# Spline and causal phases: TensorE multiplies the identity with the tokens into an unread bank at seven places

## The chip, the cores and the metric

The kernel runs on one core of a Trainium2 chip. The metric is the device time in microseconds of one execution, a median over runs. All data are float32.

## What is computed

A two-layer network over 4 x 512 tokens of 128 values. Layer 0 is half a mixture-of-experts step, a relative-position attention with 16 heads, and the mixture step again. Layer 1, on which the change bears, is cut here to its spline step and its causal step:

```python
# spline step, twice, around the causal step: x = x + 0.5 * spline(layernorm(x))
cluster_idx = argmax(calibrate(xf @ cluster_sigs.T))        # 8 clusters
sel_gates   = calibrate(xf @ sigs.T)[cluster_idx]           # 8 tiles of the chosen cluster
tile_idx    = cluster_idx * 8 + argmax(sel_gates)
comp = tanh(gelu(xf @ compress_w1 + b1) @ compress_w2 + b2)
hh   = relu(comp @ spline_w1[tile_idx] + spline_b1[tile_idx])
mag  = hh @ spline_w2[tile_idx] + spline_b2[tile_idx]
y    = layernorm(xf + mag * directions[tile_idx] * output_scale)
# causal step: x = x + causal(layernorm(x))
k, q = rotate(x @ Wk + bk), rotate(x @ Wq + bq)
wei  = softplus(causal_mask(k @ q.T / sqrt(128)))
out  = (wei @ (x @ Wv + bv)) @ Wp + bp
```

## The kernel before, in words

All tokens lie in SBUF as `x`, 16 tiles of 128 tokens by 128 values. `network` runs the phases one after the other: the layer-0 phases up to about 622 us of the profile, then `spline_phase` ("l1f0"), `causal_phase` ("l1a"), and `spline_phase` again ("l1f1"; the profile shows both spline phases under the name l1f). Each phase is a block with its own program for each engine; the engines meet at a barrier between phases. Within a phase the order on each engine is the order in which the code is written, and engines wait for one another at counted semaphores (`wait_ge`).

**A spline phase** on TensorE: `turn_tiles` transposes four normalised tiles (L2145), `score` multiplies each with 72 columns of cluster and tile signatures (L2151), `squeeze` makes the 32 hidden values of a group of four tiles (L2155). This is done for groups 0 and 1 and then for groups 2 and 3. Then `compress` (L2161) makes the two compressed values, after ScalarE's Gelu (`h_ready`). `turn_hots` (L2169) transposes the one-hot choice of tile, and `pick_parameters` (L2176) multiplies it with the table of parameters, 193 columns for each token tile.

VectorE carries the long chain: statistics, `calibrate`, `choose` and `pick_cluster` on clusters for tiles 0 to 7 (half 0) and for tiles 8 to 15 (half 1); each `pick_cluster` raises `picks_ready`. Then `calibrate`, `choose` and `mark_tiles` on the picked gates of half 0 (which raises `hot_ready`), the addition of a bias to compress's result (it waits for `comp_psum`), the same for half 1, and `magnitude` and `move_along` for each half. `calibrate` begins at L2021 and waits for ScalarE's exponential of the scores; `magnitude` begins at L2065 and waits for `par_psum`, that is for `pick_parameters`. `turn_hots(0)` waits for `hot_ready`, and `turn_hots(2)` for its second count.

ScalarE copies the transposes out of PSUM, takes the exponentials, normalises tiles 8 to 15, and computes Gelu, which is queued behind the exponential of the first picked gates.

**The causal phase** handles four batches of four tiles: `turn` (L2413) transposes, `keys_and_queries` (L2421) makes keys (n = 0) and queries (n = 1) with two 128x512 matmuls each, `values` (L2428), `score` (L2436), `gather` (L2447). VectorE's `rotate` (L2346 to L2351) waits for `kq_psum` and makes `kT` and `qT`, for which TensorE's first `score` waits.

In the profile each float32 matmul is two instructions of TensorE, a transpose is one.

Of the kernel before, what the change touches and what calls it, by code (L numbers as in the profile page):

```python
# [192 lines left out]
def attention_dram(nc):  # L193

    def dram(n, shape, dt=F32):
        return nc.dram_tensor(n, shape, dt).ap()

    return {

        "stack": [dram(f"stacked_{n}", (MARGIN + B * HEADS * 32 * FAR_PITCH,)) for n in "qk"],  # L200

        "tab": [dram(f"position_{n}", (B, TAB_SPAN)) for n in "qk"],

        "near": dram("near_terms", (B, P, 64, WIN)),
    }


def clear_semaphores(nc, sems):
# [1640 lines left out]
def spline_phase(nc, name, x, consts, lw, out=None):  # L1849


    c = consts
    HALF = TILES // 2
    N = HALF * 8
    with ExitStack() as ctx:
# [5 lines left out]
        def sem(n):  # L1861
            own_sems.append(ctx.enter_context(nc.semaphore(f"{name}_{n}")))
            return own_sems[-1]
# [22 lines left out]
        banks = ctx.enter_context(nc.psum_tensor(f"{name}_banks", [P, 8, 512], F32))  # L1886
# [11 lines left out]
        clusters_ready, picks_ready, sigs_ready = sem("clusters_ready"), sem("picks_ready"), sem("tile_sigs_ready")  # L1898
# [11 lines left out]
        with nc.Block() as block:  # L1910
# [227 lines left out]
            def _(pe):  # L2138
                def turn_tiles(g):
                    if g >= 2:  # L2140
                        pe.wait_ge(xnT_ready, g - 1)
                    for k in range(4):
                        t = 4 * g + k
                        pe.wait_ge(*((xn_by_dve, t + 1) if t < HALF else (xn_by_act, t + 1 - HALF)))
                        last = pe.transpose(psT[:, g % 2, k, :], xn[:, t, :], c["ident"][:, :])  # L2145
                    last.then_inc(xnT_psum, 1)
# [11 lines left out]
                def compress():  # L2158
                    pe.wait_ge(h_ready, 1)
                    for k in range(4):  # L2160
                        last = pe.matmul(ps_comp[:, k, :, :].rearrange("p g o -> p (g o)"), hT[:, k, :],  # L2161
                                         lw.cw2[:, :, :].rearrange("p g o -> p (g o)"), start=True, stop=True)
                    last.then_inc(comp_psum, 1)

                def turn_hots(g):
                    pe.wait_ge(*((h_ready, 1) if g < 2 else (hotT_ready, g - 1)))
                    pe.wait_ge(hot_ready, g // 2 + 1)
                    for k in range(4):
                        last = pe.transpose(ps_hot[:, g % 2, k * P:(k + 1) * P], tile_hot[:, 4 * g + k, :], c["ident"][:, :])  # L2169
                    last.then_inc(hotT_psum, 1)  # L2170

                def pick_parameters(g):

                    pe.wait_ge(hotT_ready, g + 1)
                    for t in range(4 * g, 4 * g + 4):
                        last = pe.matmul(ps_par[:, t, :], tile_hotT[:, t, :], lw.table[:, :], start=True, stop=True)  # L2176
                        if t % 2:
                            last.then_inc(par_psum, 1)

                for g in range(2):  # L2180
                    turn_tiles(g)
                score(0)
# [7 lines left out]
                squeeze(2)  # L2190
                squeeze(3)
                pe.wait_ge(xnT_ready, 4)
                compress()
                turn_hots(0)
                turn_hots(1)
                pe.wait_ge(comp_in_ready, 1)
# [13 lines left out]
def causal_phase(nc, name, x, consts, lw):  # L2210

    c = consts
    T = S // P
    with ExitStack() as ctx:
# [24 lines left out]
        ps_out = ps("ps_out", [P, S])  # L2239
# [13 lines left out]
        with nc.Block() as block:  # L2253
# [153 lines left out]
            def _(pe):  # L2407
                def turn(b):
                    if b:
                        pe.wait_ge(v_ready, b)  # L2410
                    for t in range(T * b, T * b + T):
                        pe.wait_ge(*((xn_by_dve, t + 1) if b == 0 else (xn_by_act, t + 1 - T)))
                        last = pe.transpose(ps_turn[:, (t % T) * P:(t % T + 1) * P], xn[:, t, :], c["ident"][:, :])  # L2413
                    last.then_inc(xT_psum, 1)
# [24 lines left out]
                def gather(b):  # L2439
# [8 lines left out]
                                             start=(j == 0), stop=(j == i))  # L2448
                    last.then_inc(y_psum, 1)

                turn(0)
                keys_and_queries(0, 0)
                keys_and_queries(0, 1)
# [67 lines left out]
```

## Time and profile before

| | us |
|---|---|
| median of 3 runs | 779.23 (777.95 to 779.53) |
| span of the profiled execution | 801.8 |
| TensorE busy in it | 578.0 (72%) |
| VectorE busy | 532.2 (66%) |
| ScalarE busy | 436.6 (54%) |
| mean granted TensorE clock | 0.838 |

The span runs from the first to the last instruction of one execution that was profiled; no other time is given for that execution. It is longer than the median of the timed runs, so its durations serve for differences, not for the total. The granted clock is 1.00 at 2.4 GHz and 0.50 at 1.2 GHz. The profile is read here by stretches: 622.3 to 682.4 us is the first spline phase, 682.4 to 739.6 the causal phase, 739.6 to the end the second spline phase.

### The profile page before, as it was taken

To read this page: it belongs to the slowest core of one execution; us is meant where nothing else is said; L and a number is where in the kernel's file an instruction comes from. 1 tells how busy PE (TensorE), PEld (TensorE's weight loads), DVE (VectorE), ACT (ScalarE), POOL (GpSimd) and SP (SyncE) were. 2 spreads that over 40 slices of the span, in tenths; PEclk is the share of its full clock that TensorE was granted. 3 is DMA by queue.
4 is the path that set the end of the run, shared out by engine and by line. 5 is a ranking of instruction groups with operands and counts; after the bars stand their busy time and mean duration, and the time that the engine had idled before them with its cause. 6 is when DMAs were issued, how large, how long until landed. Compare 5 with 4: busy or idle time off the path is not lost. (4 is left out here: it accounts for less than half of the span.)

```text
span 801.8 us, 16622 instructions
## 1 busy us (share of the span) xinstructions
PE 578.0 (72%) x5220; PEld 415.4 (52%) x5220; DVE 532.2 (66%) x1878; ACT 436.6 (54%) x944; POOL 225.0 (28%) x280
## 2 busy tenths in 40 slices
PE   4238964666999999999999996431994752577660
PEld 3227961233656666676667665221993542255450
DVE  7511217645778877999999985750225789666887
ACT  2004533335788888888888883610651433465522
POOL 1742443300850680094310000063342200212100
PEclk9998996976999999999999997555997555799655
DMA  8627943999999999999954406413553000000001
GB/s 249 207 92 230 277 131 101 288 317 307 265 340 360 264 303 348 255 228 309 311 125 124 126 22 191 108 48 112 172 166 89 0 1 0 1 1 1 0 1 52
DMA packets 128945, 130.79 MB, mean 163 GB/s; under 512 B 27436, under 2 KB 105116, under 8 KB 127964
## 3 DMA queue, kind: packets, MB, share of 16 engines
q1 hardware_dynamic: 122204, 101.89, 46.2%
q0 software_dynamic: 4544, 26.79, 9.0%
q10 hardware_dynamic: 2112, 1.05, 0.5%
q8 instruction: 44, 0.72, 0.4%
q14 instruction: 41, 0.34, 0.1%
HBM read 73.43 MB, written 52.92 MB: 158 GB/s over the span
## 5 line engine op out<-in xcount | busy, mean ns | idle before, releaser
L1479 DVE CUSTOM_DVE_ANT_0 l0am_prob<-l0am_ps_s,l0am_bias 128x512 f32<-128x512 f32 x256 | 161.6, 687 | 46.9 <-PE l0am_ps_s L1556 36.0
L1399 ACT ACTIVATE l0am_prob<-l0am_prob,l0am_neg_top 128x512 f32<-128x512 f32 x256 | 172.2, 730 | 11.7 <-DVE l0am_neg_top L1479 11.7
L1568 PE MATMUL l0am_ps_t<-c_ident,l0am_prob 128*128 128x128 f32 x1024 | 138.2, 279 | 0.0
L1568 PEld LDWEIGHTS l0am_ps_t<-c_ident,l0am_prob 128*128 128x128 f32 x1024 | 113.9, 142 | 16.8 <-issue 15.9
L1393 ACT COPY l0am_probT<-l0am_ps_t 128x512 f32<-128x512 f32 x128 | 69.0, 590 | 44.0 <-PE l0am_ps_t L1568 44.0
L1466 DVE COPY l0am_probT<-l0am_ps_t 128x512 f32<-128x512 f32 x128 | 82.1, 682 | 2.5 <-PE l0am_ps_t L1568 2.4
L1556 PE MATMUL l0am_ps_s<-l0am_ks,l0am_qs 32*128 32x512 f32 x512 | 73.9, 647 | 13.3 <-DVE l0am_neg_top L1479 12.1
L767 DVE COPY l0f_xsT<-l0f_psT 128x128 f32<-128x128 f32 x46 | 13.4, 292 | 104.7 <-PE l0f_psT L875 76.9
L596 ACT ACTIVATE l0f_h<-l0f_psU,l0f_experts 128x128 f32<-128x128 f32 x184 | 52.5, 368 | 40.6 <-PE l0f_psU L885 24.3
L1581 PE MATMUL l0am_ps_c<-l0am_probT,l0am_v 128*9 128x128 f32 x2048 | 67.9, 273 | 0.9 <-issue 0.9
L512 POOL DMA_INDIRECT token_results<-l0f_ys,l0f_token_i x46 | 44.3, 964 | 82.6 <-DVE l0f_ys L777 80.2
L1172 POOL TENSOR_TENSOR l0am_near<-l0am_rows_q,l0am_rows_k 128x352 f32<-128x352 f32 (+7 forms) x24 | 31.3, 1334 | 98.7 <-DMA l0am_rows_k<-position_k 98.7
L885 PE MATMUL l0f_psU<-l0f_xsT,l0f_mine 128*128 128x128 f32 x368 | 54.4, 294 | 2.8 <-DVE l0f_xsT L767 1.5
L1581 PEld LDWEIGHTS l0am_ps_c<-l0am_probT,l0am_v 128*9 128x9 f32 x2048 | 49.5, 90 | 11.7 <-issue 11.6
L1181 POOL TENSOR_TENSOR l0am_near<-l0am_rows_q,l0am_rows_k 128x192 f32<-128x192 f32 (+6 forms) x96 | 54.0, 608 | 0.2
L885 PEld LDWEIGHTS l0f_psU<-l0f_xsT,l0f_mine 128*128 128x128 f32 x368 | 47.6, 202 | 6.4 <-DVE l0f_xsT L767 2.9
L502 POOL DMA_INDIRECT sorted_tokens<-l0f_xn,l0f_pos_i x32 | 31.4, 980 | 59.1 <-DVE l0f_pos_i L668 50.2
L1556 PEld LDWEIGHTS l0am_ps_s<-l0am_ks,l0am_qs 32*128 32x128 f32 x512 | 20.2, 184 | 39.2 <-issue 24.2
L875 PE MATMUL l0f_psT<-c_ident,l0f_xs 128*128 128x128 f32 x46 | 13.4, 292 | 28.5 <-DMA l0f_xs<-sorted_tokens 27.6
L1589 PEld LDWEIGHTS l0am_ps_g<-c_ident,l0am_headT 128*128 128x128 f32 x64 | 9.0, 140 | 48.1 <-issue 28.8
L1518 PE MATMUL l0am_ps_s<-l0am_xnT,l0w_wext 128*112 128x512 f32 (+1 forms) x48 | 26.2, 709 | 5.8 <-ACT l0am_rows L1375 5.1
L1375 ACT ACTIVATE l0am_rows<-l0am_ps_s,l0w_row_bias 112x512 f32<-112x512 f32 (+1 forms) x24 | 16.1, 687 | 21.9 <-DMA stacked_q<-l0am_rows 6.8
(314 smaller groups left out, 995.6 us busy)
## 6 DMA issues: line engine op xcount, KB each, us to landing
l0am_bias<-near_terms SPq DMA_DIRECT2D x128, 192.0 KB, 5.5
near_terms<-l0am_near POOLq DMA_DIRECT2D x6, 3072.0 KB, 13.1
l0f_mine<-l0f_experts SPq DMA_DIRECT2D x46, 256.0 KB
near_terms<-l0am_near SPq DMA_DIRECT2D x2, 3072.0 KB, 10.9
l0am_rows_k<-position_k SPq DMA_DIRECT2D x12, 448.0 KB, 8.1
position_q<-l0am_rows SPq DMA_DIRECT2D x20, 224.0 KB, 5.2
position_k<-l0am_rows SPq DMA_DIRECT2D x20, 224.0 KB, 5.3
l0f_experts<-in_L_ffn_w SPq DMA_DIRECT2D x2, 2048.0 KB, 9.2
```

Source lines behind the costliest of these rows:

```text
L502: pool.indirect_dma_start(xs_dram[:, :], bass.IndirectOffsetOnAxis(ap=pos_i[:, t:t + 1], axis=0), xn[:, t, 0:XS_COLS], None).then_inc(scat ...
L512: pool.indirect_dma_start(ys_dram[:, :], bass.IndirectOffsetOnAxis(ap=token_i[:, s:s + 1], axis=0), ys[:, s % UNROLL, :], None).then_inc(y ...
L596: last = nc.scalar.activation(h[:, j, k, :], psU[:, s % 2, k, :], ACT.Gelu_apprx_tanh, bias=part_of(row, SLAB_B1 + k, 1))
L885: last = pe.matmul(psU[:, s % 2, k, :], mine[:, j, k * P:(k + 1) * P], xsT[:, j, :], start=True, stop=True)
L1181: last = engine.tensor_tensor(view(near, at, (WIN + 1, 64), (1, width)), view(rows_q, ROW_OF[pq] * 64, (1, 64), (0, width)), view(rows_k, ...
L1393: nc.scalar.copy(probT[:, u // GROUP % 2, u % GROUP, :, :], ps_t[:, u % 2, :, :]).then_inc(copied_act, 1)
L1399: nc.scalar.activation(prob[:, k, :], prob[:, k, :], ACT.Exp, bias=neg_top[:, k:k + 1], scale=-1.0)\
L1466: dve.tensor_copy(probT[:, u // GROUP % 2, u % GROUP, :, :], ps_t[:, u % 2, :, :]).then_inc(copied_dve, 1)
L1479: dve.tensor_tensor_reduce(out=prob[:, k, :], in0=ps_s[:, j, :], in1=bias[:, j, at:at + S], scale=-1.0, scalar=HUGE, op0=ALU.add, op1=ALU.min,
L1556: pe.matmul(ps_s[:, j, :], qs[r, n % 2, t * P:t * P + P], ks[r, n % 2, :], start=True, stop=True, tile_position=(32 * j, 0)).then_inc(scor ...
L1568: last = pe.transpose(ps_t[:, u % 2, i, :], prob[:, u % SLOTS_, i * P:(i + 1) * P], ident[:, :])
L1581: last = pe.matmul(ps_c[32 * j:32 * j + DH + 1, 0:P], v[:, T4 * b + i, GROUP * g + j, :], probT[:, q % 2, j, i, :], start=(i == 0), stop=( ...
```

## The change

A helper `keep_busy` issues `count` float32 matmuls of the identity (stationary) with four tiles of the tokens `x` (512 moving columns). The result goes to a PSUM bank that nothing reads before it is overwritten: bank 6 in a spline phase, `ps_out` in the causal phase. They are issued where a phase opens (3 in a spline phase, 2 in the causal one), before `compress` (4) and before the first `turn_hots` (4). The last two places also get a wait for `picks_ready`, counts 1 and 2. Nothing else is changed; no other engine's program differs.

```diff
+def keep_busy(pe, bank, ident, x, count):
+    for _ in range(count):
+        pe.matmul(bank, ident[:, :], x[:, 0:4, :].rearrange("p t d -> p (t d)"), start=True, stop=True)
...
 (spline_phase, TensorE)
+                keep_busy(pe, banks[:, 6, :], c["ident"], x, 3)
                 for g in range(2):
                     turn_tiles(g)
                 score(0)
...
                 squeeze(3)
                 pe.wait_ge(xnT_ready, 4)
+                pe.wait_ge(picks_ready, 1)
+                keep_busy(pe, banks[:, 6, :], c["ident"], x, 4)
                 compress()
+                pe.wait_ge(picks_ready, 2)
+                keep_busy(pe, banks[:, 6, :], c["ident"], x, 4)
                 turn_hots(0)
                 turn_hots(1)
...
 (causal_phase, TensorE)
+                keep_busy(pe, ps_out[:, :], c["ident"], x, 2)
                 turn(0)
                 keys_and_queries(0, 0)
```

TensorE's program of the first spline phase before, in the order in which it is issued:

```order
1037 L2145 MATMUL l1f_banks<-c_ident,l1f_xn 128x128 x8
1038 L2151 MATMUL l1f_banks<-l1w_score_w,l1f_xnT 128x72 x8
1039 L2155 MATMUL l1f_banks<-l1f_xnT,l1w_cw 32x512 x2
1040 L2145 MATMUL l1f_banks<-c_ident,l1f_xn 128x128 x8
1041 L2151 MATMUL l1f_banks<-l1w_score_w,l1f_xnT 128x72 x8
1042 L2155 MATMUL l1f_banks<-l1f_xnT,l1w_cw 32x512 x2
1043 L2161 MATMUL l1f_banks<-l1w_cw,l1f_hT 128x8 x4
1044 L2169 MATMUL l1f_banks<-c_ident,l1f_tile_hot 64x128 x8
1045 L2176 MATMUL l1f_banks<-l1w_table,l1f_tile_hotT 128x193 x8
```

And now, with the line numbers of the changed kernel:

```order
1037 L212 MATMUL l1f_banks<-x_tokens,c_ident 128x512 x3
1038 L2152 MATMUL l1f_banks<-c_ident,l1f_xn 128x128 x8
1039 L2158 MATMUL l1f_banks<-l1w_score_w,l1f_xnT 128x72 x8
1040 L2162 MATMUL l1f_banks<-l1f_xnT,l1w_cw 32x512 x2
1041 L2152 MATMUL l1f_banks<-c_ident,l1f_xn 128x128 x8
1042 L2158 MATMUL l1f_banks<-l1w_score_w,l1f_xnT 128x72 x8
1043 L2162 MATMUL l1f_banks<-l1f_xnT,l1w_cw 32x512 x2
1044 L212 MATMUL l1f_banks<-x_tokens,c_ident 128x512 x4
1045 L2168 MATMUL l1f_banks<-l1w_cw,l1f_hT 128x8 x4
1046 L212 MATMUL l1f_banks<-x_tokens,c_ident 128x512 x4
1047 L2176 MATMUL l1f_banks<-c_ident,l1f_tile_hot 64x128 x8
1048 L2183 MATMUL l1f_banks<-l1w_table,l1f_tile_hotT 128x193 x8
```

The added matmuls are the three L212 rows; all others keep their order.

## Rows read from the trace of the kernel before

**Rows 1.** Busy time by stretch; PEclk (granted clock) stands after POOL.
```profile
627.30:642.40 15.10, 15.06 (x56) 10.26 (x56) 11.13 (x38) 8.48 (x20) 1.26 (x1) 0.50 0.00 0
...
652.40:667.20 14.80, 14.62 (x48) 12.49 (x48) 11.07 (x45) 5.62 (x9) 0.00 (x0) 0.50 0.00 1
...
692.40:738.20 45.80, 36.28 (x184) 24.58 (x182) 30.58 (x66) 26.40 (x61) 6.31 (x18) 1.00 0.00 1
```

**Rows 2.** Waits in the first spline phase: us in total, times, longest.
```profile
DVE l1f_terms L2065 <- PE l1f_banks L2176: 3.1, 2, 2.4
...
DVE l1f_plus L2021 <- ACT l1f_e L1945: 2.7, 2, 1.4
```

**Rows 3.** TensorE's timeline, first spline phase: start, us, line, shapes, instructions [idle before].
```profile
627.32 2.27 PE L2145 MATMUL l1f_banks<-c_ident,l1f_xn 128*128 128x128 f32 x8 [11.65 <-DVE l1f_xn L2091]
629.37 3.55 PE L2151 MATMUL l1f_banks<-l1w_score_w,l1f_xnT 128*128 128x72 f32 x16
...
643.28 1.85 PE L2161 MATMUL l1f_banks<-l1w_cw,l1f_hT 128*128 128x8 f32 x8 [0.90 <-ACT l1f_hT L1979]
652.49 1.89 PE L2169 MATMUL l1f_banks<-c_ident,l1f_tile_hot 128*64 128x128 f32 x8 [7.36 <-DVE l1f_tile_hot L2054]
654.31 5.51 PE L2176 MATMUL l1f_banks<-l1w_table,l1f_tile_hotT 64*128 64x193 f32 x16
```

**Rows 4.** VectorE's timeline, first spline phase, same columns.
```profile
622.35 0.87 DVE L2003 BATCH_NORM_STATS2 l1f_stats<-x_tokens 128x6 f32<-128x128 f32 x4 [1.04 <-PEq L214]
...
633.28 0.20 DVE L2021 TENSOR_SCALAR l1f_plus<-l1f_e 128x64 f32<-128x64 f32 x1 [1.44 <-ACT l1f_e L1945]
...
640.88 0.20 DVE L2021 TENSOR_SCALAR l1f_plus<-l1f_e 128x64 f32<-128x64 f32 x1 [1.23 <-ACT l1f_e L1945]
...
646.18 1.07 DVE L2049 TENSOR_REDUCE l1f_picks<-l1f_masked 128x64 f32<-128x512 f32 x1
...
651.65 0.69 DVE L2054 TENSOR_TENSOR l1f_tile_hot<-l1f_chosen 128x512 f32<-128x512 f32 x1
...
656.85 0.69 DVE L2054 TENSOR_TENSOR l1f_tile_hot<-l1f_chosen 128x512 f32<-128x512 f32 x1
```

**Rows 5.** TensorE's timeline, causal phase.
```profile
686.18 1.24 PE L2413 MATMUL l1a_ps_turn<-c_ident,l1a_xn 128*128 128x128 f32 x4 [19.07 <-DVE l1a_xn L2379]
688.10 5.83 PE L2421 MATMUL l1a_ps_kq<-l1a_xnT,l1w_w_kq 128*128 128x512 f32 x8 [0.68 <-ACT l1a_xnT L2271]
...
697.25 0.66 PE L2413 MATMUL l1a_ps_turn<-c_ident,l1a_xn 128*128 128x128 f32 x4 [2.44 <-DVE l1a_v L2357]
...
703.41 1.88 PE L2421 MATMUL l1a_ps_kq<-l1a_xnT,l1w_w_kq 128*128 128x512 f32 x4
```

**Rows 6.** VectorE's timeline: starts of the causal and second spline phase; wait for the first keys.
```profile
682.45 0.87 DVE L2328 BATCH_NORM_STATS2 l1a_stats<-x_tokens 128x6 f32<-128x128 f32 x4 [0.71 <-PEq L214]
...
691.91 0.75 DVE L2346 SCALAR_TENSOR_TENSOR l1a_straight<-l1a_ps_kq,l1w_b_kq,l1w_rope 128x512 f32<-128x512 f32 x1 [2.96 <-PE l1a_ps_kq L2421]
...
739.67 0.87 DVE L2003 BATCH_NORM_STATS2 l1f_stats<-x_tokens 128x6 f32<-128x128 f32 x4 [0.81 <-PEq L214]
```

**Rows 7.** TensorE's timeline, second spline phase.
```profile
744.63 2.27 PE L2145 MATMUL l1f_banks<-c_ident,l1f_xn 128*128 128x128 f32 x8 [6.50 <-DVE l1f_xn L2091]
...
754.17 2.00 PE L2151 MATMUL l1f_banks<-l1w_score_w,l1f_xnT 128*128 128x72 f32 x16
```

**Rows 8.** Single microseconds in which the granted clock moved.
```profile
692.00:693.00 1.00, 1.00 (x3) 0.29 (x3) 1.00 (x2) 0.00 (x0) 1.00 (x2) 0.80 0.00 0
740.00:741.00 1.00, 0.00 (x0) 0.00 (x0) 0.96 (x8) 0.92 (x1) 1.00 (x2) 0.60 0.07 16
760.00:761.00 1.00, 0.53 (x5) 0.44 (x4) 0.86 (x5) 0.66 (x1) 0.00 (x0) 0.84 0.00 0
```

**Rows 9.** Attention phase, TensorE: transposes (L1568) and the microsecond behind them.
```profile
190.06 3.82 PE L1568 MATMUL l0am_ps_t<-c_ident,l0am_prob 128*128 128x128 f32 x16
...
194.00:195.00 1.00, 1.00 (x6) 0.18 (x8) 0.61 (x1) 1.00 (x2) 0.00 (x0) 0.97 0.46 197
```

## The prediction

> **What bounds the kernel now.** I read the busy time by stretch first. In the first spline phase TensorE runs at a granted clock of 0.50, its 1.2 GHz level: 15.06 us of unbroken work in the first half and 14.62 us in the second half did not raise it, while the causal phase, once warm, keeps 1.00 for 45.8 us [rows 1]. So there is something to win only where another engine waits for TensorE at the low level. The waits show how much: in the first spline phase VectorE, which carries the long chain, waits 3.1 us in two pieces for the picked parameters (2.4 and 0.7) and 2.7 us in two pieces for the exponentials of the scores [rows 2]; its timeline puts the latter two at 1.44 and 1.23 us [rows 4]. In the causal phase it waits 2.96 us for the first keys [rows 6]. Everywhere else in these phases VectorE works without a break, so a faster TensorE is worth at most 3.1 + 2.7 = 5.8 us there. The second spline phase runs alike, but for the second wait for exponentials, which it does not have. VectorE's program does not change.
>
> **What the added matmuls cost.** No such instruction is in the old trace; the nearest rows have the same shape. Two key matmuls at full clock take 1.88 us with the end of the pipeline, some 0.86 us each back to back; the first four, three fifths of them at half clock, take 5.83 us [rows 5], which fits 1.72 us at half clock. So three cost 5.2 us at half clock and 2.6 at full, four 6.9 and 3.4, two 3.4 and 1.7. Which of the two holds depends on the clock.
>
> **Where it rises and falls.** It rose to 1.00 at 692.4 us (80% over that microsecond), 4.3 us after the key matmuls began and 6.2 us after the phase's first transpose; in the second spline phase it had risen by 754.17, where 16 score instructions take 2.00 us, 9.5 us after the first transpose [rows 5, 7, 8]. It fell at 740.2, some 2 us after the causal phase's last matmul (its stretch ends at 738.2), and at 760.7, in a microsecond in which TensorE was half busy with compress [rows 1, 8]. A gap of 2.44 us ahead of 697.25 did not make it fall [rows 1, 5]. I take it that 512-column matmuls with all 128 rows raise it some 4 us after they begin, as the key matmuls did, and that gaps of 2 to 3 us can go either way.
>
> **Opening of the first spline phase.** TensorE is released with VectorE at 622.35 [rows 4]; its first transpose starts at 627.32 [rows 3]. Three added matmuls at half clock end at 622.4 + 5.2 = 627.5, or earlier if the clock rises on the way. So they delay the transposes by 0.2 us at worst and lie in TensorE's idle time of 11.65 us. The scores then cost what they cost at full clock, 2.00 us in place of 3.55 [rows 3, 7]. The transposes are paced by VectorE, so scores end near 629.4 + 2.0 = 631.4, the exponential at 631.8, and VectorE is free at 633.28 - 1.44 = 631.84: of the 1.44 us I take **1.35**. The second wait, 1.23 us, goes only if the clock survives some 3 us in which TensorE is paced by ScalarE's eight normalisations. Bounds 0 and 1.23; I take **0.6**, the middle, since the rows of gaps go both ways.
>
> **Before the picks.** The worst case first. Squeezes end at 642.4 [rows 1]. If the clock is low there, four matmuls begin at half clock, rise after 4 us and end at 642.4 + 4 + 1.4 = 647.8; compress takes 1.0 in place of 1.85 [rows 3] and ends at 648.9. The second picks were ready at 646.18 + 1.07 = 647.25 and wait for nobody; four more at full clock end at 652.3. `hot_ready` comes at 651.65 + 0.69 = 652.34 [rows 4]. So the eleven added matmuls of a phase just fit ahead of the hots, which started at 652.49 [rows 3]. Compress moves from 645.1 to 648.9; VectorE asks for it only behind `mark_tiles`, at 652.3, so this is hidden (3.4 us of cover), as is ScalarE's tanh, which follows it. From there at full clock: hots 1.0, copy 0.4, picks half of 5.51, together 4.2 in place of 7.4: ready at 656.7. VectorE is free at 656.85 + 0.69 = 657.54. The 2.4 us wait goes whole; even a delay of the hots by 0.8 us would cost nothing. The second half's hots start at 657.5 in place of 659.75: VectorE needs 6.5 us for `magnitude` and `move_along`, TensorE 7.4 at half clock and 4.2 at full, so the second wait is 0.9 or 0, against 0.7 now. Bounds -0.2 and +0.7. Together 2.2 to 3.1 us; I take **2.6** for each of the two spline phases, 5.2 in all.
>
> In the attention phase sixteen transposes, 3.82 us of nothing else, stood just ahead of a rise to 0.97 [rows 9]; so I take turns and hots as work that helps to hold the clock. The Trainium skill ("TensorE: Matmul & The Clock Gate", Part 4) says the opposite, that transposes do not count as activity for it. By that rule the clock would fall again under turns and hots, which is the second rival below (some 4 us in all, not 8.3).
>
> **Opening of the second spline phase: nothing.** The causal phase leaves the clock high until 740.2 [rows 8], and TensorE is released with VectorE at 739.67 [rows 6]. The three matmuls therefore probably run at full clock, end at 742.3 and leave a gap of 2.3 us before the transposes of 744.63 [rows 7], which are light and paced. By the rows of gaps the clock is then down again for the first scores. Bounds 0 and 1.35; I take **0**. In this phase the second pair of scores ran at full clock already [rows 7], so there is no second wait to win; if the clock is lower there by chance, 1.2 us are lost, a bound that I keep for the range.
>
> **Causal phase.** Release is at 682.45 [rows 6]; two matmuls at half clock end at 685.9, ahead of the transposes of 686.18 [rows 5]. Key matmuls from 688.1 would be at full clock: the first pair is ready after 1.8 us in place of 3.7, and VectorE, free at 691.91 - 2.96 = 688.95, starts at 689.8 in place of 691.91 [rows 6]. That is at most 2.1 us, all of it on the chain to the first scores. But the burst lasts 3.4 us where rises came after 4.3, and 2.3 us of transposes and idleness follow. Bounds 0 and 2.1; I take **1.4**, nearer the top, as the transposes add to the burst.
>
> **Sum.** 1.35 + 0.6 + 5.2 + 0 + 1.4 = 8.55, less 0.2 for the delayed transposes: 8.3 us. The profiled span of 801.8 becomes 793.5. The median of the runs is 779.23, lower than the span; I take the difference over unchanged: **770.9 us**. About 0.2% (1.6 us) is what a measurement of this kernel can tell from no change.
>
> **Rivals.**
> - *The second opening gains too.* The clock holds over gaps and light work everywhere: 1.35 x 2 + 1.2 + 3.1 x 2 + 2.1 = 12.2 us, 767.0. For it: the gap of 2.44 us that held. Against: the falls at 740.2 and 760.7. Chance 0.13.
> - *Only part of it gains.* The clock falls between the last added matmul and the picks, because the matmuls, once fast, end 1.7 us before `hot_ready` and the hots are light; or the picks, with 64 rows, do not hold it (14.62 us of them never raised it, rows 1). Then hots or half the picks gain, some 1.5 us a phase, plus one opening: 3.5 to 4.5 us, 775.2. It is also where the skill's rule on transposes leads. Chance 0.17.
> - *No gain.* TensorE speeds up, but what is won in one place is lost at the next (the second spline's lucky rise, late hots). 779. Chance 0.05.
> - *Slower: the identity does not raise the clock.* The array has 128 weights of one and otherwise zeros, and 15 us of other work did not raise it [rows 1]. Then four matmuls cost 6.9 us twice: squeezes end 642.4, compress 651.1, second burst 658.0, hots 5.5 us late, all at half clock; VectorE's wait grows from 2.4 to 7.9. With 0.2 at each opening: 2 x 5.7 = 11.4 us, 790.6. It decides from the point where the hots start over 3 us late. Against it: the key matmuls' shape is the same and they raised it. Chance 0.04.
>
> **How the numbers follow.** The forecast has 0.61. The range must leave out 2 in 10: from 766.8, the all-gain case, to 776.0, which takes in the partial case and the low bounds of both openings. Faster by over 0.2%: forecast, all-gain and partial, 0.91, less 0.02 for a partial case that shrinks below 1.6 us: 0.89. Slower: 0.04 and a share of the no-gain case, 0.05. Same: 0.06.
>
> **What would show it.** Granted clock 1.00 in the first scores of the first spline phase and VectorE's 1.44 us wait gone; both bursts before the picks at 3.4 to 5.4 us, the first ending at full clock; picks of half 0 in 2.8 us and no wait of 2.4 at the first `magnitude` in both spline phases; the second spline's first scores still at 3.55 us. I am wrong if the clock stays 0.50 under the added matmuls, if the hots start later than `hot_ready` by over 3 us, or if picks still take 5.5 us with the clock at 0.50.

## The result, and the profile after

The changed kernel takes 771.54 us in the median of 4 runs (767.23 to 774.42) against 779.38 us (777.95 to 779.79, also 4 runs) for the kernel before: a ratio of 0.9893, 95% interval 0.9856 to 0.9931, so 7.8 us less. The profiled execution took 770.1 us with a span of 768.4.

The span of before's profile was 801.8, and only part of those 33.4 us belongs to the change: 24.1 lie ahead of the first spline phase, which begins at 622.35 there [rows 4] and at 598.23 here. That part holds none of the edit, and a second profile of the kernel before (the first experiment) begins that phase at 597.11. The comparison that counts is by phase, first statistics to first statistics. The busy time by stretch of the changed kernel has the three phases in this order; columns are length, busy time of TensorE, its weight loads, VectorE, ScalarE and GpSimd, granted clock, DMA share, GB/s:

```profile
598.23:652.72 54.49, 36.35 (x134) 21.70 (x135) 50.15 (x186) 23.43 (x50) 4.97 (x4) 0.72 0.00 1
652.72:708.38 55.66, 44.98 (x196) 28.17 (x197) 38.20 (x104) 31.21 (x74) 10.17 (x21) 0.93 0.00 1
708.38:768.40 60.02, 35.93 (x134) 23.36 (x134) 49.83 (x185) 23.49 (x49) 4.97 (x4) 0.70 0.06 18
```

Before, they were 60.10, 57.22 and 62.13 long by the same cuts, with clocks of 0.50, 0.91 and 0.56. So the phases give 5.61 + 1.56 + 2.11 = 9.3 us in this execution. VectorE's busy time is nearly what it was (50.15 us against 50.02 in the first spline phase): what went is waiting.

TensorE's timeline of the first spline phase (start, us, line, shapes, instructions, idle before in brackets), where L212 is the added matmul:

```profile
598.23 4.94 PE L212 MATMUL l1f_banks<-x_tokens,c_ident 128*128 128x512 f32 x6 [6.69 <-PEq L221]
...
605.15 1.95 PE L2158 MATMUL l1f_banks<-l1w_score_w,l1f_xnT 128*128 128x72 f32 x16
...
611.46 2.54 PE L2158 MATMUL l1f_banks<-l1w_score_w,l1f_xnT 128*128 128x72 f32 x16
...
615.78 5.57 PE L212 MATMUL l1f_banks<-x_tokens,c_ident 128*128 128x512 f32 x8
...
622.00 3.68 PE L212 MATMUL l1f_banks<-x_tokens,c_ident 128*128 128x512 f32 x8
625.99 1.03 PE L2176 MATMUL l1f_banks<-c_ident,l1f_tile_hot 128*64 128x128 f32 x8 [0.31 <-DVE l1f_tile_hot L2061]
627.35 2.85 PE L2183 MATMUL l1f_banks<-l1w_table,l1f_tile_hotT 64*128 64x193 f32 x16 [0.32 <-ACT l1f_tile_hotT L1962]
...
632.55 4.82 PE L2183 MATMUL l1f_banks<-l1w_table,l1f_tile_hotT 64*128 64x193 f32 x16 [0.32 <-ACT l1f_tile_hotT L1962]
```

The first scores take 1.95 us where they took 3.55 [rows 3]. The clock falls in the middle of the second scores (2.54, between 2.00 and 3.69), the first burst brings it back (5.57), the second runs at full clock throughout (3.68), hots and the first picks follow at full clock (2.85 against 5.51). In the second picks it falls again (4.82).

No long gap stands ahead of the fall in the second scores. The first of the four microseconds before it, and the one in which the clock moved, columns as above:

```profile
608.00:609.00 1.00, 0.70 (x4) 0.28 (x2) 0.96 (x2) 1.00 (x4) 1.00 (x1) 1.00 0.00 0
...
612.00:613.00 1.00, 1.00 (x11) 1.00 (x9) 0.90 (x5) 0.29 (x1) 0.00 (x0) 0.88 0.00 0
```

TensorE was busy for 0.70, 0.73, 0.89 and 0.87 of the microseconds from 608 to 612, paced by ScalarE, and never idle for more than 0.30 us at a time. On VectorE every wait of [rows 2] is gone; the rows that had them have no bracket:

```profile
607.63 0.19 DVE L2028 TENSOR_SCALAR l1f_plus<-l1f_e 128x64 f32<-128x64 f32 x1
...
614.39 0.18 DVE L2028 TENSOR_SCALAR l1f_plus<-l1f_e 128x64 f32<-128x64 f32 x1
...
630.97 0.28 DVE L2072 TENSOR_TENSOR l1f_terms<-l1f_banks,l1f_comp 128x128 f32<-128x128 f32 x1
...
637.41 0.29 DVE L2072 TENSOR_TENSOR l1f_terms<-l1f_banks,l1f_comp 128x128 f32<-128x128 f32 x1
```

One VectorE instruction became slower, `reach` in `calibrate`. It and GpSimd's addition of two tensors next to it, before and then after:

```profile
634.10 0.63 DVE L2025 SCALAR_TENSOR_TENSOR l1f_reach<-l1f_sig,c_segment_ids 128x448 f32<-128x448 f32 x1
...
631.91 1.26 POOL L1928 TENSOR_TENSOR l1f_x_shifted<-x_tokens,l1w_beta 128x512 f32<-128x512 f32 x1 [5.87 <-DVE l1f_newton L2016]
```

```profile
608.44 1.10 DVE L2032 SCALAR_TENSOR_TENSOR l1f_reach<-l1f_sig,c_segment_ids 128x448 f32<-128x448 f32 x1
...
607.79 1.27 POOL L1935 TENSOR_TENSOR l1f_x_shifted<-x_tokens,l1w_beta 128x512 f32<-128x512 f32 x1 [5.86 <-DVE l1f_newton L2023]
```

Before, GpSimd was done at 633.17, ahead of `reach`. With the first wait for exponentials gone, `reach` starts while GpSimd still adds (607.79 to 609.06) and takes 0.47 us more.

The causal phase, first on TensorE and then on VectorE:

```profile
652.72 3.75 PE L212 MATMUL l1a_ps_out<-x_tokens,c_ident 128*128 128x512 f32 x4 [15.35 <-PEq L221]
...
658.23 3.70 PE L2433 MATMUL l1a_ps_kq<-l1a_xnT,l1w_w_kq 128*128 128x512 f32 x8 [0.68 <-ACT l1a_xnT L2283]
...
665.98 0.66 PE L2425 MATMUL l1a_ps_turn<-c_ident,l1a_xn 128*128 128x128 f32 x4 [3.16 <-DVE l1a_v L2369]
666.47 2.30 PE L2448 MATMUL l1a_ps_wei<-l1a_kT,l1a_qT 128*128 128x512 f32 x4
```

```profile
660.25 0.75 DVE L2358 SCALAR_TENSOR_TENSOR l1a_straight<-l1a_ps_kq,l1w_b_kq,l1w_rope 128x512 f32<-128x512 f32 x1 [1.03 <-PE l1a_ps_kq L2433]
...
661.70 0.69 DVE L2363 TENSOR_TENSOR l1a_kT<-l1a_straight,l1a_crossed 128x512 f32<-128x512 f32 x1
...
663.74 1.58 DVE L2363 TENSOR_TENSOR l1a_qT<-l1a_straight,l1a_crossed 128x512 f32<-128x512 f32 x1
```

The eight key instructions take 3.70 us, not 5.83 [rows 5], and VectorE's wait for the first keys is 1.03, not 2.96 [rows 6]. VectorE starts them 7.53 us into the phase instead of 9.46, 1.93 earlier. Some of it is given back in a sum of two operands (kT and qT: 0.69 + 1.58 = 2.27 us; they took 1.19 + 0.69 = 1.88 before), which leaves 1.54 of the phase's 1.56.

The second spline phase on TensorE, and VectorE's two waits that are left in it:

```profile
708.38 2.81 PE L212 MATMUL l1f_banks<-x_tokens,c_ident 128*128 128x512 f32 x6 [1.53 <-PEq L221]
713.35 2.27 PE L2152 MATMUL l1f_banks<-c_ident,l1f_xn 128*128 128x128 f32 x8 [2.15 <-DVE l1f_xn L2098]
715.41 3.53 PE L2158 MATMUL l1f_banks<-l1w_score_w,l1f_xnT 128*128 128x72 f32 x16
...
731.99 5.40 PE L212 MATMUL l1f_banks<-x_tokens,c_ident 128*128 128x512 f32 x8 [1.72 <-DVE l1f_picks L2056]
...
738.59 2.85 PE L2183 MATMUL l1f_banks<-l1w_table,l1f_tile_hotT 64*128 64x193 f32 x16 [0.33 <-ACT l1f_tile_hotT L1962]
...
744.15 5.51 PE L2183 MATMUL l1f_banks<-l1w_table,l1f_tile_hotT 64*128 64x193 f32 x16
```

```profile
719.30 0.20 DVE L2028 TENSOR_SCALAR l1f_plus<-l1f_e 128x64 f32<-128x64 f32 x1 [1.43 <-ACT l1f_e L1952]
...
749.70 0.29 DVE L2072 TENSOR_TENSOR l1f_terms<-l1f_banks,l1f_comp 128x128 f32<-128x128 f32 x1 [1.02 <-PE l1f_banks L2183]
```

The opening runs at full clock, ends 2.15 us ahead of the transposes, and the first scores are at half clock as before. The wait of 2.39 for the first picks is gone, the one for the second has grown from 0.69 to 1.02. Here the two bursts are the other way round: the first runs at full clock (3.67 us), then come 0.95 us of compress and a gap of 1.72, the clock falls (0.62 over the microsecond from 732), and the second burst takes 5.40. It still ends just in time: `hot_ready` comes at 737.04 and the hots start at 737.23.

### The profile page after: what moved, and what is told of

Its sections match the earlier page's. It is cut to its first block and busy times, and to the rows that moved or that the text cites. A ratio compares the mean times of both kernels' runs of the same rounds, so it can differ in the third digit from the quotient of the medians.

```text
span 768.4 us, 16718 instructions
## 1 busy us (share of the span) xinstructions
PE 595.7 (78%) x5268; PEld 415.3 (54%) x5268; DVE 531.5 (69%) x1878; ACT 436.5 (57%) x944; POOL 225.4 (29%) x280
## 5 line engine op out<-in xcount | busy, mean ns | idle before, releaser
L212 PE MATMUL l1f_banks<-x_tokens,c_ident 128*128 128x512 f32 x44 | 26.1, 746 | 9.9 <-PEq L221 8.2
L903 PE MATMUL l0f_psR<-l0f_experts,l0f_h 128*128 x192 | 27.1, 286 | 1.9 <-ACT l0f_h L603 1.9
```

## The experiments

Theory A: the added matmuls raise TensorE's clock (from 1.2 to 2.4 GHz), and the time goes where VectorE waited for TensorE. Theory B: the two new waits on `picks_ready` reorder TensorE's work, and that is what pays. Theory C: the gain is a matter of chip or run, as the 24 us ahead of the phases suggest. Edits are shown against the changed kernel.

**The kernel before, once more.**

> The kernel before, unchanged, for a second profile. The profile of before had a span of 801.8 us where its timed runs had a median of 779.4, and the changed kernel's span was 768.4, 1.7 us under its own time of 770.1. Theory (clock under the added matmuls explains the whole difference): the stretch from the first spline phase's first statistics to the end is again 179 to 181 us (before 179.4, changed 170.2), and the 22 us too much lie ahead of it and are absent here, so the span is about 778. Rival (something ahead of the spline phases differs between the two kernels): the span is again near 800, or the earlier part is over 2 us longer than the 598.2 us of the changed kernel.

Measured: 779.01 us against 779.51, ratio 0.9999 (0.9979 to 1.0019). Span 776.6; the phases are 60.11, 57.26 and 62.12 long, within 0.04 us of the first profile, and begin at 597.11, not 622.35. So the phases can be compared across profiles and the part ahead of them can't: on the two chips on which the kernel before takes 779 us it is 596.36 to 601.52 us long in the eight profiles taken there, and the medians below carry this spread. Theory C is right about the 24 us and falls for the 9.3.

**One part at a time.** Openings of the spline phases alone:

```
-                pe.wait_ge(picks_ready, 1)
-                keep_busy(pe, banks[:, 6, :], c["ident"], x, 4)
...
-                pe.wait_ge(picks_ready, 2)
-                keep_busy(pe, banks[:, 6, :], c["ident"], x, 4)
...
-                keep_busy(pe, ps_out[:, :], c["ident"], x, 2)
```

> Only the three matmuls at the opening of each spline phase. Theory: first wait for the exponentials gone in the first spline phase, second perhaps, 1.3 to 2.6 us; nothing in the second spline phase, where the matmuls run at full clock and leave a gap; sum 1.3 to 2.6 us, 777. Nothing at the picks: the wait of 2.4 us stays in both. Rival (the opening's rise carries over to the picks): over 4 us.

Waits and bursts ahead of the picks alone:

```
-                keep_busy(pe, banks[:, 6, :], c["ident"], x, 3)
...
-                keep_busy(pe, ps_out[:, :], c["ident"], x, 2)
```

> Only the two waits and the two bursts of four ahead of compress and of the first hots, in both spline phases. Theory: the 2.4 and 0.7 us waits for picked parameters shrink to under 1 us together in each spline phase, 4.4 to 6.2 us in all, 774. Both waits for exponentials stay. In the first spline phase the bursts start at half clock, and the hots start within 0.5 us of tile_hot. Rival (the bursts delay the hots as much as the clock gives back): within 1.5 us of before.

The causal opening alone (both of the above taken out, the last `keep_busy` kept):

> Only the two matmuls at the opening of the causal phase. Theory: VectorE's wait for the first keys falls from 3.0 to about 1.0 us, causal phase 1.4 to 2.1 us shorter, 777.6. Where the clock does not rise in time: no gain, 0.0 and not slower, since the matmuls end before the first transposes. Rival: the causal phase is bound by ScalarE after its first batch, so the early keys are absorbed and the phase is not shorter than 0.5 us.

The waits on `picks_ready` without any matmul (all four `keep_busy` calls taken out):

> The two waits for picks_ready stay, every added matmul is left out. Theory: the waits cost nothing and give nothing, since compress may end up to 7 us later and the hots wait for a later semaphore anyway; stretch from the first spline phase to the end 179.5 us as before, ratio 1.000. Rival (the second wait, which holds compress back from VectorE's bias addition, costs): 0.5 us or more in a spline phase.

What they gave, with the changed kernel and the kernel before. Ratios are to the kernel before on the same chip; the last three columns are phase lengths of the profiled execution:

| kernel | ratio (95%) | spline 1 | causal | spline 2 |
|---|---|---|---|---|
| before, once more | 0.9999 (0.9979 to 1.0019) | 60.11 | 57.26 | 62.12 |
| changed | 0.9893 (0.9856 to 0.9931) | 54.49 | 55.66 | 60.02 |
| openings alone | 0.9980 (0.9951 to 1.0008) | 58.55 | 57.21 | 61.96 |
| before the picks alone | 0.9923 (0.9895 to 0.9951) | 58.69 | 57.41 | 62.11 |
| causal alone | 0.9996 (0.9977 to 1.0015) | 60.11 | 56.88 | 62.20 |
| waits alone | 0.9994 (0.9968 to 1.0020) | 60.09 | 57.26 | 62.19 |

Theory B falls: the waits alone leave every phase as it was. Of 779 us the ratios make 1.6, 6.0 and 0.3 us of the three parts, 7.9 in all against 8.3 for the whole, so they roughly add up, each uncertain by 1.5 to 3 us; the first and the third alone lie within the noise.

*Openings.* The first wait for exponentials is gone (1.44 before), as the prediction has it. The second shrinks to 0.74. `reach` takes 1.10 us here too. VectorE comes to the first exponentials 1.53 us earlier in the phase, 0.49 of the second wait is gone and 0.47 is lost in `reach`: 1.55, which is what the phase is shorter by. TensorE and VectorE of this kernel:

```profile
610.11 3.39 PE L2158 MATMUL l1f_banks<-l1w_score_w,l1f_xnT 128*128 128x72 f32 x16
```

```profile
613.86 0.20 DVE L2028 TENSOR_SCALAR l1f_plus<-l1f_e 128x64 f32<-128x64 f32 x1 [0.74 <-ACT l1f_e L1952]
```

The second scores run mostly at half clock here (3.39), where the same program in the changed kernel had 2.54 and no wait. Nothing in the phase that differs between the two kernels has run by then. The repetition of the changed kernel below took 3.69 at this place, so when the clock falls is not the program's alone to decide.

*Before the picks.* The profile taken is of one of the two slowest of its 12 executions (779.43 us; the median is 774.05). Its TensorE shows why that one gained little:

```profile
619.47 4.83 PE L212 MATMUL l1f_banks<-x_tokens,c_ident 128*128 128x512 f32 x8
...
624.94 3.68 PE L212 MATMUL l1f_banks<-x_tokens,c_ident 128*128 128x512 f32 x8
...
631.02 4.53 PE L2183 MATMUL l1f_banks<-l1w_table,l1f_tile_hotT 64*128 64x193 f32 x16 [0.32 <-ACT l1f_tile_hotT L1962]
```

Both bursts do what they do in the changed kernel, even without the opening; then the clock falls in the middle of the picks, and VectorE waits 0.95 us where it waited 2.39. That is the "only part gains" rival, in one execution. In its second spline phase the picks' wait is shorter by 1.39 too, and a wait of 1.24 for the second exponentials appears, which the kernel before did not have there (its second scores ran at full clock, [rows 7]). The mean granted clock is on record for every execution: it was 0.849 in this one, the lowest of the twelve, and 0.864 to 0.877 in nine of them, where the 35 executions of the kernel before had 0.836 to 0.857. So such an execution is the rare case, and the median gain of 6.0 us goes with a higher clock, as theory A has it; which waits went in the faster ones no profile shows.

*Causal opening.* The keys come as in the changed kernel (the wait is 1.02), but the phase gains 0.34, not the 1.4 to 2.1 that were expected. TensorE and VectorE:

```profile
670.88 1.02 PE L2420 MATMUL l1a_ps_turn<-c_ident,l1a_xn 128*128 128x128 f32 x4 [3.15 <-DVE l1a_v L2364]
671.70 3.03 PE L2443 MATMUL l1a_ps_wei<-l1a_kT,l1a_qT 128*128 128x512 f32 x4
```

```profile
676.02 0.16 DVE L2344 TENSOR_TENSOR l1a_newton<-l1a_newton 128x4 f32<-128x4 f32 x1 [3.14 <-ACT l1a_newton L2268]
```

By finishing early TensorE has made its own gap longer, 3.15 us against 2.44 [rows 5], and the clock falls right behind it. The first causal scores take 3.03 (1.67 before), ScalarE is late, and VectorE's wait for ScalarE's root grows from 1.93 to 3.14: 1.21 us given back. With 0.38 lost in the sums beside GpSimd (kT and qT take 2.26), 0.33 is left of 1.92. The size is that of the expectation's rival (ScalarE absorbs the early keys, not over 0.5), but ScalarE is late because the scores ran at half clock. The changed kernel had the same gap (3.16), but the clock fell only inside the scores (2.30), and its wait stayed 1.93.

**Half the rows.** The slower rival was that the added matmuls cost their time and raise no clock. A matmul with 64 rows takes the same time (a burst of four at full clock 3.67 us here and 3.67 or 3.68 with 128 rows):

```
-        pe.matmul(bank, ident[:, :], x[:, 0:4, :].rearrange("p t d -> p (t d)"), start=True, stop=True)
+        pe.matmul(bank, ident[0:64, :], x[0:64, 0:4, :].rearrange("p t d -> p (t d)"), start=True, stop=True)
```

> The changed kernel with the added matmuls on 64 of the 128 rows, same 512 columns, same number, same places: the same time on the array, less of it active. Theory (what counts is that full-height matmuls raise the clock; 64-row picks never did in 5.5 us): the clock stays at 0.50 under them, so this is my slower case: two bursts of 6.9 us end 5.5 us after tile_hot, VectorE's first wait for picked parameters grows from 2.4 to 7.9 us, 11 us slower than before, 790. Rival (any dense stream raises it): as the changed kernel, 771.

Measured: 784.88 us, ratio 1.0062 (1.0032 to 1.0092), slower than before; phases 61.01, 57.29, 62.78. Two stretches of its busy time, the opening and the second burst, and its rows of the picks on both engines:

```profile
601.50:606.90 5.40, 5.38 (x6) 1.83 (x6) 5.10 (x33) 1.78 (x3) 3.70 (x3) 0.50 0.00 2
...
625.50:632.50 7.00, 7.00 (x8) 2.43 (x8) 6.50 (x17) 0.26 (x1) 0.00 (x0) 0.50 0.00 0
```

```profile
634.40 5.51 PE L2183 MATMUL l1f_banks<-l1w_table,l1f_tile_hotT 64*128 64x193 f32 x16
```

```profile
640.03 0.29 DVE L2072 TENSOR_TENSOR l1f_terms<-l1f_banks,l1f_comp 128x128 f32<-128x128 f32 x1 [4.34 <-PE l1f_banks L2183]
```

TensorE is busy without a break in both, at 0.50. The second burst ends late, hots and picks follow at half clock, and the wait for the picks grows from 2.39 to 4.34 (3.01 in the second spline phase). The rival's mechanism is real. It stays smaller than the 11.4 us worked out for it, since the clock had risen between: the second scores took 2.00 us and removed their own wait, and the first burst cost 3.67 and not 6.9. The medians give 4.8 us, the phases of this execution 1.6; this execution was also 4.4 us longer ahead of the phases than that of the kernel before (601.52 against 597.11), where nothing is edited, so only the 1.6 us are shown to be the rows' doing.

**Transposes in place of matmuls.** Each added matmul becomes eight transposes of 128x128, about the same time:

```
-        pe.matmul(bank, ident[:, :], x[:, 0:4, :].rearrange("p t d -> p (t d)"), start=True, stop=True)
+        for k in range(8):
+            pe.transpose(bank[:, (k % 4) * P:(k % 4 + 1) * P], x[:, k % 4, :], ident[:, :])
```

> The changed kernel with each added matmul replaced by eight transposes of 128x128 tokens back to back, the same time on the array at either clock (0.21 us each at half). My theory: transposes raise and hold the clock too, since sixteen of them stood ahead of a rise in the attention phase; as the changed kernel, 770 to 774. Rival (transposes do not count as activity): the clock stays at 0.50 and it is as with half the rows, 790.

Measured: 773.6 us, ratio 0.9925 (0.9892 to 0.9958); phases 54.44, 56.04 and 58.68. The profiled execution is the fastest of its nine (767.84 us). The stretches of the opening, of scores and squeezes, and of everything up to the second picks:

```profile
597.00:602.00 5.00, 5.00 (x25) 4.96 (x25) 4.72 (x31) 1.69 (x3) 3.64 (x3) 0.52 0.01 2
602.00:613.00 11.00, 10.18 (x58) 6.12 (x56) 9.81 (x34) 6.91 (x18) 1.26 (x1) 1.00 0.01 1
613.40:633.00 19.60, 14.77 (x115) 13.73 (x116) 18.26 (x51) 8.69 (x12) 0.00 (x0) 1.00 0.00 0
```

Transposes alone take the clock from 0.50 to 1.00 at the end of the first stretch, and it stays at 1.00 over the transposes, scores, squeezes and picks that follow. The Trainium skill ("TensorE: Matmul & The Clock Gate", Part 4) has them not count as activity for the clock; this trace, of float32 transposes, does not agree, and its numbers decide.

**More matmuls, where the trace still shows waits.** Ten more, at six places: two ahead of the second spline's transposes (behind `std_ready`), in each spline phase two ahead of the turns of the second half and one between the picks of the first half and the hots of the second, and two ahead of the causal phase's second turn:

```
                 keep_busy(pe, banks[:, 6, :], c["ident"], x, 3)
+                if out is not None:
+                    pe.wait_ge(std_ready, 1)
+                    keep_busy(pe, banks[:, 6, :], c["ident"], x, 2)
...
                 squeeze(1)
+                keep_busy(pe, banks[:, 6, :], c["ident"], x, 2)
...
                 pick_parameters(1)
+                keep_busy(pe, banks[:, 4, :], c["ident"], x, 1)
                 turn_hots(2)
...
                 values(0)
+                keep_busy(pe, ps_out[:, :], c["ident"], x, 2)
                 turn(1)
```

> The changed kernel plus matmuls where its trace shows the clock falling in idle time: two in the second spline phase's opening behind std_ready, two ahead of turns 2 and 3, one between the picks of the first half and the second hots (bank 4, free there), two in the causal phase ahead of turn 1. Theory: the second spline phase's wait of 1.43 us for exponentials and its 1.02 us wait for picks go, the causal phase gains 0.5, the luck at the second exponentials goes (1.2 us in unlucky runs): 2.5 to 4 us below the changed kernel, 768, and a narrower spread. Rival (the added ones delay turns and hots by as much): the same as the changed kernel or 1 to 2 us slower.

Measured: 768.05 us (767.1 to 774.21), ratio 0.9858 (0.9812 to 0.9904); phases 54.44, 56.04, 57.80: 168.28 us in all against 170.17. The busy time of the second spline phase up to its last picks, and TensorE's rows of the first scores and of the last picks there:

```profile
711.10:747.00 35.90, 31.40 (x138) 18.46 (x139) 33.06 (x115) 17.46 (x33) 4.97 (x4) 1.00 0.00 1
```

```profile
718.03 1.95 PE L2158 MATMUL l1f_banks<-l1w_score_w,l1f_xnT 128*128 128x72 f32 x16
...
745.43 2.85 PE L2183 MATMUL l1f_banks<-l1w_table,l1f_tile_hotT 64*128 64x193 f32 x16 [0.32 <-ACT l1f_tile_hotT L1962]
```

The clock is 1.00 over the whole stretch, and VectorE has no wait for TensorE or for exponentials in either spline phase. The gap between the bursts is 1.71 us here, as long as in the changed kernel, and the clock holds over it. In the causal phase, though, one of VectorE's sums falls beside GpSimd's bias additions and takes 1.81 us, not 0.69:

```profile
664.18 1.81 DVE L2368 TENSOR_TENSOR l1a_kT<-l1a_straight,l1a_crossed 128x512 f32<-128x512 f32 x1
```

Keys start 1.78 us earlier than before, kT and qT take 2.50 us and not 1.88, which leaves 1.16 of the phase's 1.18.

**Both versions, again, and two of the causal phase.** All four ran on one chip, on which the kernel before took 801.64 us (794.75 to 808.05): every kernel's stretch ahead of the phases is 618.8 to 624.0 long there. First the changed kernel, unchanged:

> The changed kernel once more, beside the versions with more matmuls. Theory (its time depends on where rises and falls of the clock happen to lie, so runs of the same kernel differ in which waits return): median 771 to 773, single runs spread over 5 us or more, and a trace whose waits differ from those of the first one: one or two of the four places (first exponentials and second picks of the second spline phase, second exponentials, causal keys) other than before. Rival: the same waits as in the first trace.

The version with more matmuls, unchanged (its matmuls stand at six added places, not seven):

> The version with seven added places more a second time, for its ratio on the same chip as the changed kernel. Theory: 768 to 770, 2 to 4 us below the changed kernel, the same trace as the first (no wait for TensorE in either spline phase). Rival: the first time was a lucky draw of six runs; no different from the changed kernel.

The causal phase alone, with its opening and two matmuls to fill the gap (both spline parts taken out):

```
                 values(0)
+                keep_busy(pe, ps_out[:, :], c["ident"], x, 2)
                 turn(1)
```

> Only the causal phase: two matmuls at its opening and two ahead of turn 1, where TensorE idles 3.2 us for VectorE. With the opening alone the clock fell in that gap and the first scores took 3.0 in place of 1.7 us, so that the phase won only 0.4 of the 1.9 us that the keys came earlier. Theory: the clock holds over the gap, the phase is 1.0 to 1.5 us shorter than 57.2, that is 55.8 to 56.2. Rival (ScalarE's chain, not the clock, swallows the early keys): again only 0.4 us, 56.9.

The version with more matmuls, with GpSimd's additions moved behind VectorE's first sums:

```
-                pool.wait_ge(var_ready, 3)
+                pool.wait_ge(v_ready, 1)
...
+                    if b == 0:
+                        dve.wait_ge(x_biased_ready, 4)
...
-                dve.wait_ge(x_biased_ready, 4)
```

> The version with more matmuls, and GpSimd's four additions of the output bias to the tokens (5.0 to 5.5 us) start behind VectorE's values instead of beside its rotations; VectorE waits for them ahead of the first add_y instead of ahead of the first weigh. In the trace the addition that makes kT took 1.81 us beside GpSimd, 0.69 where GpSimd is idle. Theory: kT and qT back to 0.69 each, causal phase 1.1 us shorter, 54.9. Rival: the same slowing falls on VectorE's instructions behind it (statistics, weigh), and the phase stays at 56.0.

| kernel | median us | ratio (95%) | spline 1 | causal | spline 2 |
|---|---|---|---|---|---|
| changed, again | 795.10 | 0.9907 (0.9876 to 0.9938) | 55.60 | 56.05 | 59.89 |
| more, again | 791.76 | 0.9884 (0.9837 to 0.9930) | 54.45 | 55.70 | 57.87 |
| causal, gap filled | 800.43 | 0.9986 (0.9955 to 1.0018) | 58.78 | 57.27 | 62.18 |
| more, GpSimd moved | 792.98 | 0.9908 (0.9872 to 0.9944) | 54.46 | 59.00 | 57.83 |

The change's gain repeats. Here its second scores ran at half clock from the start (3.69 us), and a wait of 1.03 for the second exponentials is back, which makes the first spline phase 1.1 us longer. The version with more matmuls had the shortest three phases of all profiles, both times (168.28 and 168.02), and the lower median both times. It beats the kernel before. Its interval overlaps that of the change each time, so an advantage over the change (1.9 and 3.5 us shorter phases, 3.3 us by the medians on this chip) is likely and not shown.

*Causal, gap filled.* No gain in its phase, where 55.8 to 56.2 us were expected and 56.9 by the rival. The gap is down to 1.28 us and the clock holds over it; but this time the rise came late:

```profile
686.10 5.32 PE L2428 MATMUL l1a_ps_kq<-l1a_xnT,l1w_w_kq 128*128 128x512 f32 x8 [0.67 <-ACT l1a_xnT L2278]
```

The wait for the keys is 2.79. So this execution doesn't tell whether early keys and a held clock together give the whole gain. (That the first spline phase is 1.3 us shorter, with no edit in it, is the clock again: its second wait for exponentials happened to be absent.)

*GpSimd moved.* kT is back at 0.69, as expected, but the phase is 3.0 us longer than with more matmuls before (59.00 against 56.04), where the theory had 54.9 and the rival 56.0. VectorE and GpSimd:

```profile
685.69 1.27 DVE L2355 SCALAR_TENSOR_TENSOR l1a_newton<-l1a_mv,l1a_newton 128x4 f32<-128x4 f32 x1
686.99 1.23 DVE L2356 TENSOR_SCALAR l1a_newton<-l1a_newton 128x4 f32<-128x4 f32 x1
```

```profile
685.67 5.02 POOL L2330 TENSOR_TENSOR l1a_x_biased<-x_tokens,l1w_b_p 128x512 f32<-128x512 f32 x4 [56.01 <-DVE l1a_v L2374]
```

Four steps of Newton's iteration on 128x4 values, 0.16 or 0.17 us each elsewhere, now take 1.27, 1.23, 1.22 and 1.18, each about as long as one of GpSimd's four additions (5.02 / 4 = 1.25). That adds 4.2 us, of which VectorE's wait for ScalarE behind them swallows 1.3 (0.60 left of 1.93). TensorE idles 4.68 us ahead of the next scores and meets them at half clock (1.19 us for two instructions, 0.67 before), so that VectorE waits 1.14 us for the next keys, where it had no wait.

The Trainium skill ("GPSIMD Engine Reference", Specifications) says that GpSimd shares its SBUF interfaces with VectorE and contends with VectorE's instructions that have two SBUF inputs or run in a 2-port perf mode. The traces agree as far as instructions of two SBUF inputs are slowed (the sums take 1.58 and 1.81 us, not 0.69, and `reach` 1.10, not 0.63), while in the changed kernel the products of L2358, with one operand in PSUM, keep their 0.75 us beside GpSimd. But not every such sum is hit: the kT of 661.70 above ran beside GpSimd at 0.69. And an instruction of four elements per row pays as much as one of 512, the one at 686.99 with its single tensor input too; no run shows in which mode that one ran.

## Why the prediction held, step by step

- **Opening of the first spline phase, 1.35: right about the wait, with a term missing.** The first wait for exponentials went from 1.44 to 0 in the changed kernel, its repetition and the version with the openings alone. But in all three, and wherever else this wait went, `reach` then ran beside GpSimd and took 1.10 us, not 0.63. VectorE comes to the first exponentials 1.53 us earlier (9.40 us into the phase, 10.93 before) and loses 0.47 of it: 1.06. The 0.2 us for delayed transposes did not come: they start 4.97 us into the phase before and after.
- **The second wait there, 0.6 between 0 and 1.23: the size is a matter of luck.** What was left of it was 0 in the changed kernel, 1.03 in its repetition and 0.74 with the openings alone. The profile showed the lucky end; from three executions the middle seems the better forecast.
- **Before the picks, 2.6 in each spline phase: right in mechanism and nearly in size.** The 2.39 wait went whole in both phases. The second went to 0 in the first phase and 1.02 in the second, where I had given 0.9 or 0. With it the first phase gains 3.08 there and the second 2.39 - 0.33 = 2.06, 5.1 in all against 5.2. The worst case that I worked out for the bursts (5.4 and 3.4 us) is what came in the first phase: 5.57 and 3.68, ending at 625.7 just ahead of `hot_ready` at 625.8. In the second phase the first burst was the fast one and the clock fell between the two (3.67 and 5.40), which no step of mine had; the second ended about when `hot_ready` came, and the hots started 0.19 us behind it, against 0.15 in the first phase.
- **Opening of the second spline phase, 0: right, and by its steps.** 2.81 us at full clock, a gap of 2.15, scores at 3.53. The version with more matmuls closes that gap and the wait of 1.43 is gone.
- **Causal phase, 1.4: right in size here (1.56), with a term missing.** I had taken two thirds of 2.1, for the chance that the clock rises late. It rose in time, and keys came 1.93 us earlier; 0.39 was then lost in a sum that ran beside GpSimd, which no step of mine had. The two versions with the causal part alone show two more ways to lose it: a clock that falls in the longer gap (0.34 kept), and a late rise (nothing kept). By itself the part can't be told from nothing (0.9996, or 0.3 us, with an interval to 0.9977, or 1.8 us). So 1.4 is probably too much for an average execution of the part alone, but it lies inside the interval.
- **The sum.** 8.3 us against 9.3 in the trace and 7.8 by the medians. What I had put at the middle (the second wait) came out at its top in the profiled execution; in the repetition, where that wait is back, the phases give 179.45 - 171.54 = 7.9. That the total came so near is in part luck: two losses to GpSimd (0.47 and 0.39), which I did not have, stand against a second wait that went whole. And the 7.8 us of the medians have an interval of 5.4 to 11.2 by their ratio, wider than the 1.6 us that I had said a measurement could tell.
- **A reading that was wrong.** I wrote that VectorE works without a break everywhere else. It does not: in the spline phases it waits 0.61 us for ScalarE's root, and in the causal phase 1.93 and three times 2.37 us for ScalarE and up to 1.61 us for TensorE at full clock. The bound of 5.8 us for the first spline phase survives this (5.61 were won); in the causal phase the wait of 1.93 is the one that grew to 3.14 where the clock fell.
- **The rivals.** "Only part of it gains" occurs in single executions, but not as the usual case, and the skill's rule on transposes, which I had set beside it, is not borne out here. "The second opening gains too" needs two more matmuls behind `std_ready`. "Slower" needs a matmul that does not raise the clock: half the rows made it, and the time was lost at the place described, the picks' wait, with much less than the size (1.6 us in the phases, 4.8 by the medians, against 11.4).

## What to carry to other kernels

Where an engine on the long chain waits for TensorE and the granted clock in that stretch is 0.50 however busy TensorE is, matmuls whose result nobody reads, put into its idle time so that they end just ahead of the work that is waited for, can give that engine its waits back; count beforehand whether they still end in time at half clock. A gap behind them may or may not let the clock fall (it held over gaps of 1.71, 2.44 and 3.40 us, and fell behind gaps of 1.72, 2.15 and 3.15), and so may paced work without any gap over 0.3 us, so look at each such stretch: the version with two more matmuls in one (behind `std_ready`) is the one in which the second opening paid. And when work is pulled forward, look at what it now runs beside: here a gain of 1.9 us met GpSimd and lost 0.4 to 0.6, and one of 1.5 lost 0.47.

## What the runs showed of the hardware that I had not expected

- Twenty-four transposes of 128x128 in float32, back to back for 5 us, raise the clock as well as full-height matmuls do; 5.4 and 7.0 us of unbroken matmuls with 64 rows leave it at 0.50.
- The clock fell while TensorE was busy for 0.70 to 0.89 of each microsecond with no idle time over 0.30 us (608 to 612 us of the changed kernel, the fall 0.8 us later); in its repetition it held over a gap of 3.40 us and the causal scores behind it (1.67 us).
- The same instructions at the same place meet a different clock from one execution to the next: the second scores of the first spline phase took 2.54 us in one execution of the changed kernel and 3.69 in another.
- VectorE instructions of 128x4 values took 1.2 us, not 0.17, while GpSimd added two tensors in SBUF; one of 128x448 took 1.10, not 0.63, in every profile in which it ran beside such an addition.
- The same program took 22 us longer on one chip than on another (801.64 against 779.23). The four profiles taken there, of other versions, have it ahead of the phases studied (618.8 to 624.0 us long against 596.4 to 601.5); what makes it so was not tried.
